# Reordering the third feed-forward's routing, shared chunks and scatters in a four-layer kernel

## The reference, cut to what matters

```python
xn = _layernorm(x)
scores = sigmoid(xn @ gate_w)                        # 32 experts
topk_w, topk_i = top_k(scores, 6)                    # 6 of 32 for each token
topk_w = topk_w / (sum(topk_w) + 1e-20)
act    = silu(xn @ wg[e]) * (xn @ wu[e])             # 256 -> 96
routed = sum over the 6 experts of topk_w * (act @ wd[e])   # 96 -> 256
shared = (silu(xn @ sg) * (xn @ su)) @ sd            # 256 -> 192 -> 256, for every token
x = x + 0.5 * (routed + shared)
```

## Time and profile before

| what | us |
|---|---|
| median of 3 runs | 1376.55 |
| the profiled execution | 1378.79 |
| its span, first to last instruction | 1376.9 |
| TensorE busy in the span | 1142.0 (83%) |
| VectorE busy | 751.9 (55%) |
| GpSimd busy | 582.8 (42%) |
| ScalarE busy | 484.9 (35%) |

### The profile page before, as it was taken

One profiled execution on the slowest core, in us unless ns is written; L12 is line 12 of the kernel. 1 busy time (PEld: TensorE's weight loads), 2 busy tenths in 40 slices (PEclk: granted clock), 3 DMA queues, 4 the chain that ended last, 5 costly groups with the idle time before them and its releaser, 6 DMA issues.

```text
span 1376.9 us, 19454 instructions
## 1 busy us (share of the span) xinstructions
PE 1142.0 (83%) x5926; PEld 931.2 (68%) x5926; DVE 751.9 (55%) x2317; ACT 484.9 (35%) x934; POOL 582.8 (42%) x571
## 2 busy tenths in 40 slices
PE   4699997688898998997365599999988675999994
PEld 3587775366577886776244489998654463899993
DVE  4663356454645554356624184777767552556665
ACT  2222343255534432343231144444242211344441
POOL 3680134221203222135777402767506767006766
PEclk9999999799989999999586799999998778899997
DMA  9621443940000045753422466987302222568987
GB/s 325 249 77 39 130 127 96 335 154 1 0 0 31 32 177 189 268 189 104 134 100 95 175 192 207 271 278 241 115 1 83 101 89 96 168 188 271 281 275 219
DMA packets 125154, 210.03 MB, mean 153 GB/s; under 512 B 15280, under 2 KB 104752, under 8 KB 123184
## 3 DMA queue, kind: packets, MB, share of 16 engines
q1 hardware_dynamic: 100480, 141.64, 31.0%
q0 software_dynamic: 24576, 67.14, 15.4%
HBM read 129.56 MB, written 101.19 MB: 168 GB/s over the span
## 4 chain that ended last, share of the span: by engine, by line
PE 59%; POOL 11%; DVE 10%; issue 9%; ACT 5%; DMA 4%; SPq 1%; POOLq 0%; ACTq 0%; DVEq 0%
PE ps L828 17%; PE ps L838 11%; POOL xd L588 9%; PE ps L746 6%; PE ps L799 5%; PE ps L1104 4%; PE ps L758 4%; PE ps L809 3%; PE ps L970 2%; PE ps L977 2%; ACT xnt L1212 2%; DMA G<-yd,slot_of 1%; POOL G L602 1%; DMA xd_in<-xd 1%; PE ps L887 1%
## 5 line engine op out<-in xcount | busy, mean ns | idle before, releaser
L602 POOL DMA_INDIRECT G<-yd,slot_of x256 | 249.6, 975 | 365.8 <-DMA yd<-yo 269.5
L588 POOL DMA_INDIRECT xd<-xnt,slot_of x256 | 254.8, 995 | 193.3 <-DVE slot_of L1751 110.0
L828 PE MATMUL ps<-WE,xT 128*128 x1016 | 189.6, 331 | 0.1
L1345 ACT ACTIVATE xT<-ps 128x512 f32<-128x512 f32 (+1 forms) x168 | 99.3, 591 | 214.2 <-PE ps L799 213.2
L1861 DVE TENSOR_TENSOR hid<-hid,ps 128x192 f32<-128x192 f32 (+2 forms) x168 | 65.4, 390 | 183.7 <-ACT hid L1364 183.1
L828 PEld LDWEIGHTS ps<-WE,xT 128*128 128x128 f32 x1016 | 165.3, 193 | 0.6 <-issue 0.4
L1868 DVE COPY yo<-ps 128x512 f32<-128x512 f32 (+1 forms) x168 | 114.7, 684 | 62.1 <-PE ps L838 62.1
L1840 DVE SCALAR_TENSOR_TENSOR XT<-G,wt,XT 128x256 f32<-128x256 f32 x256 | 124.7, 488 | 43.4 <-DMA G<-yd,slot_of 31.2
L799 PE MATMUL ps<-ident,xd_in 128*128 128x128 f32 x664 | 103.2, 278 | 36.7 <-DMA xd_in<-xd 31.1
L1231 ACT ACTIVATE S<-ps 128x512 f32<-128x512 f32 (+1 forms) x72 | 42.8, 594 | 254.7 <-PE ps L746 252.4
L838 PE MATMUL ps<-WE,hT 96*128 x508 | 130.9, 380 | 0.0
(11 more groups left out here) (225 smaller groups left out, 1895.5 us busy)
## 6 DMA issues: line engine op xcount, KB each, us to landing
xd_in<-xd SPq DMA_DIRECT2D x164, 256.0 KB, 3.9
yd<-yo SPq DMA_DIRECT2D x164, 256.0 KB, 3.0
WE<-w SPq DMA_DIRECT2D x8, 1280.0 KB, 7.5
W0E<-w0e SPq DMA_DIRECT2D x2, 4864.0 KB, 24.2
xd<-xnt,slot_of POOLq DMA_INDIRECT x256, 2.4
G<-yd,slot_of POOLq DMA_INDIRECT x256, 3.7
XT<-x_in SPq DMA_DIRECT2D x4, 512.0 KB, 6.1
out<-XT SPq DMA_DIRECT2D x16, 128.0 KB, 3.4
```

What stands on the lines that cost most here:

```text
L588: nc.gpsimd.indirect_dma_start(xd[f // 2][:, :], bass.IndirectOffsetOnAxis(ap=slot_of[:, t, k:k + 1], axis=0), xnt[:, t, :], None).then_in ...
L602: nc.gpsimd.indirect_dma_start(G[:, n % G_RING, :], None, yd[f // 2][0:min(ly.early[t] * 2, ly.TILES) * P, :], bass.IndirectOffsetOnAxis(a ...
L828: last = mm(dst, xT[:, q % 2, a, k, :], flat[:, bass.ds(expert[2 * q + a] + k * 2 * ly.H, 2 * ly.H)], start=(k == 0), stop=(k == KD - 1))
L1345: fn(xT[:, q % 2, 0:m].rearrange("p a k t -> p (a k t)"), ps[:, TX, 0:m * D], ACT.Copy).then_inc(TL.xT, 1)
```

## The change

In the table of chunks, both chunks of a block of FF2 had the bank pair 2 and 3; now they alternate between 2 and 3, and 6 and 7, as in FF3. On GpSimd the scatter of FF2's tile 0 moves ahead of block 1's power, and the gathers of FF1's tiles 8 and 9 move behind it. On TensorE, ScalarE and VectorE block 3 is routed directly behind block 2, ahead of the splitting of the shared weights and of all shared chunks. No instruction is added or removed.

```diff
     for f in (2, 3):
         for b in range(NB):
-            add(("s", f, b), "s1", f, b, SH1, (2,) if f == 2 else (2, 6))
+            add(("s", f, b), "s1", f, b, SH1, (2, 6))
 ...
# GpSimd
-            for t in range(10):
+            for t in range(8):
                 gather(1, t)
-                if t in (3, 7):
-                    inverse(F_NORM[2], t // NT)
+                if t == 3:
+                    inverse(F_NORM[2], 0)
             scatter_tile(2, 0)
-            gather(1, 10)
+            inverse(F_NORM[2], 1)
+            for t in (8, 9, 10):
+                gather(1, t)
             scatter_tile(2, 1)
             gather(1, 11)
             gather(1, 12)
 ...
# TensorE, prepare2
                 route_rank(2)
-                shared(2, 0)
                 route_turn(3)
                 route_logits(3)
+                route_rank(3)
+                shared(2, 0)
                 shared(2, 1)
-                route_rank(3)
                 shared(2, 2)
 ...
# ScalarE, prepare2
                 score(2, 2, TURN2)
+                std(F_NORM[2], 3)
+                routed_rows(3)
+                route_plain(3)
+                score(2, 3, TURN2)
                 act.wait_ge(sh1_in, 16 * SH1)
 ...
                 shared(2, 0)
                 route_split(1)
-                std(F_NORM[2], 3)
-                routed_rows(3)
-                route_plain(3)
-                score(2, 3, TURN2)
                 shared(2, 1)
 ...
# VectorE, prepare2
                 gathered_all(1, 4 * NG - 2)
+                route_stats(3)
+                offsets(F_NORM[2], 3, True)
+                chosen(2, 3)
+                route_slots(3)
                 for c in range(SH1):
 ...
                 route_low(0)
-                route_stats(3)
                 shared(2, 0)
                 route_low(1)
-                offsets(F_NORM[2], 3, True)
-                chosen(2, 3)
                 shared(2, 1)
-                route_slots(3)
                 route_low(2)
```

## The result

The changed kernel takes 1370.24 us, the median of 6 runs (1366.95 to 1372.31), beside 1376.55 for the kernel before on the same chip. The ratio is 0.9954, with a 95% interval from 0.9940 to 0.9968: 6.3 us faster (4.4 to 8.3). Forecast was 1369.4, range 1367.8 to 1373.2. The profiled execution took 1370.14 us, its span is 1368.3, and the granted clock of TensorE over it is 0.907, where it was 0.915.

The account below looks back on a forecast made before the run. GpSimd's unbroken run of indirect DMAs was taken to bound the seam between FF1 and FF2. Moving six scatters saves 7.65 us less 0.5 for a late power, taken as 7.1: 1376.55 - 7.1 = 1369.4 us, range 1367.8 to 1373.2.

Parts of the forecast that it names:

- GpSimd's run sets the seam: Between FF1 and FF2, GpSimd's unbroken indirect DMAs set the time; the other engines have some 10 us to spare.
- 6 x 1.275 us leave the run: Tile 0's six scatters move into GpSimd's wait before block 1's power, taking 7.65 us out of its unbroken run.
- The power 0.5 us late: Block 1's power on GpSimd starts 0.5 us later behind the six scatters, leaving a net gain of 7.1 us.
- rival 3: Six scatters beside FF1's pairs run at the longest row's pace, delaying block 1's power: 3.8 us gain, 1372.7 us; 8%.
- The gathers' waits go: VectorE's two waits for tile 11's gathers near FF1's end, 1.38 and 1.46 us, vanish; VectorE is 2.3 us earlier.
- block 3's slots at 704.5: Block 3, routed directly behind block 2, has its scatter slots at 704.5 us, 21.0 us after its variance at 683.5.
- first chunk at 709.3: FF2's first shared chunk starts on TensorE at 709.3 us, after routing and splitting, where it could at 686.6 before.
- The chunks' end at 772.3: FF2's four shared blocks, 16.0 us each without the 1.49 us wait, take 63.0 us and end at 772.3, as before.
- The spare time: FF2's shared chunks end 3 us before the table's first rows arrive at 775.4, or 10 us by FF3's pace.
- Rivals 1 and 2: FF2's shared chunks become the bound: in part, 1373.0 us, 11%; or at TensorE's lower clock throughout, 1387 us, 5%.
- Nothing counted behind the seam: After the seam everything shifts as one; some 1.5 us possible from TensorE's clock in FF2's pairs was not counted.

Follow-up runs that it names:

- e5: Kernel before with only GpSimd's new order (tile 0's scatters ahead of block 1's power); 1370.09 us, ratio 0.9952 to the kernel before.
- e6: Changed kernel with GpSimd's old order, so only block 3's earlier routing and two bank pairs; 1376.61 us, ratio 0.9990 to the kernel before.
- e7: Changed kernel with FF2's shared chunks on one bank pair again; 1368.36 us, ratio 0.9944 to the kernel before.
- e8: Changed kernel with block 1's power as a root on ScalarE and the splits ahead of block 2's scoring; 1369.13 us, ratio 0.9950.
- e9: Changed kernel without the scatters of FF2's last two tiles (12 of 96); 1556.49 us in a slow set, ratio 0.9955 to the kernel before.
- e11: Changed kernel with FF2's low parts written as zeros, not by VectorE subtractions of two SBUF inputs; 1562.24 us in a slow set, ratio 1.0022.
- e3: The changed kernel once more, nothing else altered; 1577.72 us in a slow set, ratio 1.0026 to the kernel before.
- e12: Changed kernel with one bank pair for FF2's chunks and block 1's power as a root on ScalarE and VectorE; 1579.78 us, slow set, ratio 1.0104.
- e1: Kernel before with only GpSimd's new order; 1571.41 us in a slow set, ratio 0.9986 to the kernel before.
- e4: Changed kernel with FF2's shared chunks on one bank pair again; 1586.76 us in a slow set, ratio 1.0092 to the kernel before.
- e2: Changed kernel with GpSimd's old order, so only routing and bank pairs changed; 1589.57 us in a slow set, ratio 1.0122 to the kernel before.

## Why the prediction was right, and where its terms were not

The mechanism is the one forecast, by its own steps:

- **GpSimd's run sets the seam.** Right. e5 moves only GpSimd's instructions and is 6.3 us under before; e6 moves all the rest and gains nothing.
- **6 x 1.275 us leave the run.** Right in after: 138.57 us were measured and 138.6 forecast for what is left. But that took the lengthening of some DMAs (below) as a constant. It was 2.3 us before and in after, and is 4.95, 4.2 and 5.05 us in e5, e7 and e8 (the DMAs over 1.05 us, less 0.97 each). In e5 the run from the gather behind the power takes 141.1 us, in e7 140.3, in e8 141.1. That after had before's 2.3 us again was luck: the profiles differ by 2.7 us in it, and the forecast had no term for it.
- **The power 0.5 us late.** This term was too small. Measured, in before's frame by block 0's power, it is 1.73 us in after, 1.26 in e5 and 1.27 in e7. Two parts. The first scatter starts 0.77 us behind the slot write that frees it (620.40 to 621.17) where the earlier trace rows gave 0.28, and 0.47 us and not 0.30 pass before the second; both are the same in every profile with early scatters. That makes GpSimd free 0.7 to 0.9 us later than forecast. In after, TensorE also ran one `down` of an expert slowly (3.72 us at 621.76, and 1.99 in before, e5, e7 and e8 at that place): the granted clock from 621 to 626 us is 0.58, and 1.00 in those four. Block 1's variance then came 1.7 us late. It isn't the scatters alone: e5, e7, e8, e9 and e11 run the same early scatters with 1.99 us. But it isn't the chance of one execution either: e3, the changed kernel again, has 3.76 us there and e12 too, e1 and e4 have 2.4, and e2, without early scatters, has 2.54. What brings the lower clock there stays open; e9 and e11 are the changed kernel up to that place, so it varies from one execution to another.
- **Scatters beside FF1's pairs (rival 3).** Did not happen. The six take 7.58 us in after, 7.68 in e5, the longest 1.07.
- **The gathers' waits go, block 3's slots at 704.5, first chunk at 709.3.** In before's frame 705.5 (the end of the write, which the forecast went by) and 709.95, with the late power in them. Right.
- **The chunks' end at 772.3.** It came 2.0 us late: 772.27, in before's frame 774.3. 0.65 us of that is the later start; the rest is in the chunks, 62.92 us to the end of the last `down` where 61.6 were forecast. A block was put at 16.0 us and took 16.2, 16.5 and 16.0, but not as 5.38 + 3.01 + 2.0 + 3.14 + 2.5: it had 7.3 to 8.6 us for the 24 matmuls, and 4.05 to 4.62 us for `down`, except in the first block. The wait went, and by e7 half or more of what it gave came back as slower matmuls at a lower granted clock (0.77 in after, 0.87 in e7).
- **The spare time.** Forecast 3.1 us between the experts' row and the first turn; 774.62 - 772.27 = 2.35 us are left, since the chunks were 2.0 and the turn 1.3 us late. Rivals 1 and 2 did not happen, but chunks that end 2.4 us later would have cost time.
- **Two slips in the working.** For rival 3 six scatters of 1.80 us from 622.71 end at 633.2 and not 633.5, when the 0.30 us behind the last is taken off as in the forecast: 3.55 us late, a gain of 4.1 and a time of 1372.4. And in the table of slices TensorE is busy at 3 to 7 tenths from 620 to 790 us, not at 6 to 7. Neither changes the forecast.
- **Nothing counted behind the seam.** In after it was 0.57 us of gain. From SyncE's read to the first gather of FF2 it is 69.5 us before, and 69.9, 69.0 and 69.7 in after, e5 and e7. The first stretch of the pairs ran at clock 0.50, not higher than before's 0.67, and cost nothing that shows.

The sum. In the four profiles with early scatters, by SyncE's read in before's frame, the seam gained 5.98 (after), 3.9 (e5), 4.7 (e7) and 4.9 us (e8), 4.9 on average, where 7.1 were forecast. Two terms account for that: 7.7 less the 1.73 of the late power in after, and 5.2 less 1.26 in e5, where the run got only 5.2 us shorter. The medians say 6.3, 6.3, 8.0 and 7.3, each to about 2 us. The spans of e5, e7 and e8 are shorter than before's by another 3.4 to 5.5 us behind the read, where nothing was changed (in e7 and e8 some 4 us of it behind the second of attention's powers, which GpSimd computes between FF2's gathers; in e5 most of it ahead of that); and the profiled execution of before was itself 2.24 us above its median. So the forecast from the median came out within 0.8 us, while its one term was 1 to 3 us too large in each profile: the mechanism is right, and that the number came so near is in part luck. What makes up the difference between seam and median, I can't say from single executions: it stays open.

The fastest version is e7: the changed order on GpSimd and the routing, over one bank pair, 1368.36 us. Against the changed kernel that is not a difference to rely on, since the intervals overlap (0.9928 to 0.9960, and 0.9940 to 0.9968), and its profile is shorter by 3.9 us of which none lies in the seam (SyncE's read is later than after's, at 772.59). e6 and e7 together show that the bank pairs need not be there.

## What to carry to other kernels

Where one engine issues without a break and stands waiting just before, look for work that is ready inside the wait and of a length that fits: of the first 7.65 us of work moved in, 3.9 to 6.0 us were won at the seam, and one more tile, in a single profile, won nothing and lengthened a later wait. It pays only while that engine's run ends last: in the sets near 1575 us the chunks ended last, and the same edit showed no gain. Take the price of the wait's end from a row at the same place, not from another stage. And a wait removed on TensorE is not its own length: 2.2 to 3.0 us of 6.0 came out, and the same matmuls took 2.9 to 3.6 us longer at a lower granted clock.

## What the runs showed of the hardware

**Indirect DMAs are longer beside some VectorE instructions.** Six profiles (before, after, e5 to e8) hold 672 indirect DMAs of FF1's end and FF2. Count as a neighbour every row of VectorE's timeline over 1 us, one instruction or two of the same line on end, that overlaps the DMA. Of 153 DMAs beside a row with two inputs in SBUF, 58 take over 1.05 us, up to 1.95. Where every such row beside it reads PSUM (`finish`), it is none of 22, the longest 0.97. Beside neither, 2 of 497, up to 1.17. The rows of e5 above show two neighbours: 701.15 is 0.97 and 702.43 is 1.94; here is VectorE at that time, the first instruction reading PSUM, the second not.

```profile
701.17 1.23 DVE L1823 SCALAR_TENSOR_TENSOR XT<-ps,XT 128x1024 f32<-128x1024 f32 x1 [2.45 <-PE ps L760]
702.31 1.21 DVE L1961 TENSOR_TENSOR XHe<-X,XHe 128x1024 fp32r<-128x1024 f32 x1
```

In e11, without such instructions in the chunks, one of 76 is long (1.17), and in e3, at the same speed of the chip, 3 of 74 are, up to 1.86. That agrees, but with few cases, and it decides neither for the theory nor for the rival (five or more stay), since e3 had only three. The Trainium skill has a rule of this kind ("SBUF — State Buffer", "SBUF: two separate sides"): GpSimd and VectorE have a port pair in common, which one of them holds exclusively, VectorE with two SBUF inputs against a GpSimd operation that reads SBUF; and it gives a DMA issued by GpSimd that grows from about 620 to 3100 ns beside a VectorE copy. Here the growth was at most 0.98 us and on average 0.14 us for a DMA so placed, not a factor of 5. The prediction weighed this rule for six scatters; the long DMAs lie in the whole run, 2.3 to 5 us of them, and their spread was the part I left out.

**A gap of 2.60 us tied to a place in the program.** GpSimd stands still for 2.59 or 2.60 us once among FF2's scatters, always in front of the 75th of the 96 (749.92 before, 741.95 after, 743.57, 749.41, 742.43 and 743.46 in e5 to e8), whatever the time. In e9, with 12 scatters fewer at the end, it is the 75th again (778.69), and among FF3's scatters the 57th has such a gap in all six profiles (1115.43 before, 1107.20 after). The cause isn't shown.

**The same kernel at 1376 and at 1573 us.** The kernel before is the same in all three sets, and the second and the third set ran on one chip. The waits of e3 show where some of the time is: a VectorE instruction behind 45.3 us of "issue", a ScalarE instruction behind 32.0 us of "remote". What else the chip did then isn't to be seen in a trace of one core.
